# Norm statistics a stage ahead, square roots on ScalarE, weight packing beside the shared expert, a residual sum in the experts' stage, fp8 scaling on ScalarE

## The reference, cut to what matters

```python
# L0: cross-attention, 16 heads, then 8 experts with a capacity, top 2
Q = split_heads(query, 16) * dh ** (-0.5)
weights = softmax(einsum('bhqd,bhkd->bhqk', Q, Kh) + b + MASK_VALUE * (1.0 - valid))
out = einsum('bhqk,bhkd->bhqd', weights, Vh)
...
scores = softmax(xf @ router_w); expert_weights, top_experts = top_k(scores, 2)
out = out + y * expert_weights[:, k][:, None]        # y: gelu(xe @ w1) @ w2, per expert
...
# L1: rms norm, linear, "depool" add; then 8 gated experts (top 2) and one shared gated expert
sg = sigmoid(x @ shared_gate_w); so = silu(x @ sw_gate) * (x @ sw_up) @ sw_down
out = out + sg * so
# L2: cross-attention and self-attention, 4 experts of several layers; the norm ahead of them is an rms norm
# L3: projected attention, then a linear layer on fp8-rounded inputs and weights
```

## Time and profile before

| | us |
|---|---|
| device time, median of 3 runs (range) | 3182.69 (3179.83 to 3188.03) |
| the profiled execution, its own time | 3181.22 |
| its span | 3179.5 |
| PE busy in it | 2534.5 (80%) |
| DVE busy | 2180.8 (69%) |
| ACT busy | 1264.9 (40%) |
| POOL busy | 996.3 (31%) |

### The profile page before, as it was taken

One profiled execution on the slowest core, in us unless ns is written; L12 is line 12 of the kernel. 1 busy time (PEld: TensorE's weight loads), 2 busy tenths in 40 slices (PEclk: granted clock), 3 DMA queues, 4 the chain that ended last, 5 costly groups with the idle time before them and its releaser, 6 DMA issues. The chain is left out here.

```text
span 3179.5 us, 57281 instructions
## 1 busy us (share of the span) xinstructions
PE 2534.5 (80%) x21348; PEld 1651.8 (52%) x21348; DVE 2180.8 (69%) x5526; ACT 1264.9 (40%) x2260; POOL 996.3 (31%) x1420
## 2 busy tenths in 40 slices
PE   2997285999904497997989876886799999969972
PEld 1443263666603266886556543444466555656662
DVE  6897763666547764766678767997666545867758
ACT  1786353333212313111346654773322222256621
POOL 3442271110066170112656316874000000024330
PEclk9999597999956599998999987998899999989996
DMA  4331266221171026665721022100100000011001
GB/s 104 122 120 58 91 237 203 80 73 63 45 249 31 24 97 233 234 224 185 243 78 48 18 72 82 43 23 6 64 9 12 1 1 1 1 42 52 22 9 58
DMA packets 158167, 266.90 MB, mean 84 GB/s; under 512 B 22635, under 2 KB 106137, under 8 KB 151876
## 3 DMA queue, kind: packets, MB, share of 16 engines
q1 hardware_dynamic: 131204, 186.97, 17.8%
q0 software_dynamic: 17904, 76.23, 7.1%
q10 hardware_dynamic: 8784, 0.04, 0.2%
HBM read 175.25 MB, written 88.34 MB: 83 GB/s over the span
## 5 line engine op out<-in xcount | busy, mean ns | idle before, releaser
L1427 ACT ACTIVATE l2e_hf<-l2e_H 128x512 f32<-128x512 f32 x208 | 124.2, 597 | 376.1 <-PE l2e_H L1383 376.1
L1552 POOL TENSOR_TENSOR all_m_rstd<-all_m_sq,all_mhalf 128x8 f32<-128x8 f32 x18 | 29.6, 1646 | 551.0 <-DVE all_m_sq L1537 550.9
L731 DVE TENSOR_REDUCE l0a_mx<-l0a_S 128x2 f16<-128x512 f32 x256 | 168.3, 688 | 24.0 <-PE l0a_S L565 23.3
L1463 DVE CAST l2e_hh<-l2e_hf 128x512 f16<-128x512 f32 x208 | 88.8, 427 | 125.8 <-ACT l2e_hf L1427 110.7
L727 DVE CUSTOM_DVE_ANT_0 l2s_masked<-l2s_S,l2s_mq 128x128 f32<-128x128 f32 (+1 forms) x512 | 153.2, 349 | 19.9 <-PE l2s_S L565 19.5
L680 ACT ACTIVATE l0a_pf<-l0a_ST 128x512 f32<-128x512 f32 x256 | 146.7, 602 | 45.3 <-PE l0a_ST L579 45.0
L1383 PE MATMUL l2e_H<-l2o_hi,l2e_w 128*128 128x512 f16 x576 | 151.8, 382 | 14.9 <-DVE l2e_w L1439 14.9
L1427 ACT ACTIVATE l0e_hf<-l0e_H 128x512 f32<-128x512 f32 x128 | 76.4, 597 | 207.2 <-PE l0e_H L1383 207.2
L1383 PE MATMUL l2e_H<-l2e_hh,l2e_w 128*128 128x512 f16 x640 | 155.1, 379 | 0.0
L1383 PE MATMUL l1e_H<-l1b_hi,l1e_w 128*128 128x256 f16 (+1 forms) x936 | 144.7, 274 | 7.8 <-DMA l1e_w<-packed,all_second_weight_row 7.8
L1465 DVE TENSOR_TENSOR l2e_hl<-l2e_hf,l2e_hh 128x512 f16<-128x512 f32 x208 | 144.0, 693 | 7.2
(11 more groups left out here) (713 smaller groups left out, 7541.3 us busy)
## 6 DMA issues: line engine op xcount, KB each, us to landing
l0e_wf<-in_L_ffn_w SPq DMA_DIRECT2D x16, 1024.0 KB, 7.2
rows<-l0a_zeros SPq DMA_DIRECT2D x16, 640.0 KB, 5.9
l1u_rb<-rows SPq DMA_DIRECT2D x20, 512.0 KB, 5.2
results<-l1e_y SPq DMA_DIRECT2D x39, 256.0 KB, 3.8
l0a_kv<-in_ctx SPq DMA_DIRECT2D x16, 512.0 KB, 4.1
rows<-l0a_zeros SPq DMA_DIRECT2D x16, 512.0 KB, 4.9
l0d_p_cx<-in_ctx SPq DMA_DIRECT2D x16, 512.0 KB, 6.7
l0u_rb<-rows SPq DMA_DIRECT2D x16, 512.0 KB, 5.7
```

Source lines behind the costliest of these rows:

```text
L731: m = nc.vector.tensor_reduce(mx[h % 2][:, :, i], ps[:, :].rearrange("p (u k) -> p u k", u=TB), AX.X, ALU.max)
L1427: nc.scalar.activation(hf[q % 4][0:fn, :], pair_of(q, lay)[0][0:fn, :], lay.func, scale=1.0 / WS).then_inc(acted, 1)
L1463: nc.vector.tensor_copy(high, v).then_inc(hi_done, 1)
L1552: self.nc.gpsimd.tensor_tensor(out=(self.rstd, self.rstd2)[which][:, g], in0=(self.sq, self.sq2)[which][:, g], in1=self.g.mhalf[:, 0:self. ...
```

## The change

1. `load` works out the statistics of `l0n` on DVE at its end, waiting for x a quarter at a time, and three roots on POOL; SP no longer waits for x. `l0n` is built with `given=True`.
2. `l0a` is given `Moments`: in slots 2 and 3 of every second step from j = 6 DVE does BN_STATS of one tile of x and BN_AGGR of the one before, POOL three roots; `l0gn` is built with `given=True`.
3. `l1n` no longer packs weights. Its 8 roots go from POOL to ACT (`Sqrt`) with a reciprocal and one Newton step on DVE (`invert`, 5 small ops for each root).
4. `l1s` packs the weights of experts 4 to 7 instead: one of the four after each pair of down units, the high part on ACT, the low part on DVE behind the adds of the unit a = 0, loads and stores on SP, whose end waits for the last store.
5. `l2w` no longer adds `l2o_xin` to x on POOL; POOL does the 32 adds at the start of `l2e`, where DVE's first adds wait for them (`poured`).
6. `fp` multiplies by the scale on ACT instead of DVE, four times 128 x 2048, into two buffers.

```diff
+    def invert(self, dve, which, q):
+        if self.by_act:
+            nc, g = self.nc, slice(q * self.GQ, (q + 1) * self.GQ)
+            a, r, w = (self.sq, self.sq2)[which][:, g], (self.rstd, self.rstd2)[which][:, g], self.turn[:, g]
+            dve.wait_ge(self.rooted_in[which], q + 1)
+            self.then(dve, nc.vector.reciprocal(r, r))
+            self.then(dve, nc.vector.tensor_tensor(w, r, r, ALU.mult))
+            self.then(dve, nc.vector.tensor_tensor(w, w, a, ALU.mult))
+            self.then(dve, nc.vector.tensor_scalar(w, w, -0.5, 1.5, ALU.mult, ALU.add))
+            nc.vector.tensor_tensor(r, r, w, ALU.mult).then_inc(self.roots[which], 1)
...
             self.statistics(dve, q)
             if q >= 1:
+                self.invert(dve, 0, q - 1)
                 self.second(dve, q - 1)
             if q >= 2:
+                self.invert(dve, 1, q - 2)
                 self.apply(dve, q - 2)
         after(dve)
+        self.invert(dve, 0, 3)
         self.second(dve, 3)
         self.lo_parts(dve, 0)
+        self.invert(dve, 1, 2)
         self.apply(dve, 2)
         self.lo_parts(dve, 1)
+        self.invert(dve, 1, 3)
         self.apply(dve, 3)
...
+                for q in range(4):
+                    dve.wait_ge(x_in[q], 16)
+                    for t in range(8 * q, 8 * q + 8):
+                        moments.tile(dve, t)
+                moments.gather(dve, NT - 1)
...
+                if pack is not None:
+                    pack.begin_move(sp)
+                    pack.load(sp, 0)
+                    pack.load(sp, 1)
+                    for e in range(pack.experts):
+                        pack.store(sp, e)
+                        if e + 2 < pack.experts:
+                            pack.load(sp, e + 2)
+                    pack.end_move(sp)
...
+                for t in range(NT if pour is not None else 0):
+                    nc.gpsimd.tensor_tensor(out=g.x[:, t, :], in0=g.x[:, t, :], in1=pour[:, t, :], op=ALU.add
+                                            ).then_inc(poured, 1)
...
                             row = t - un.n * tiles
+                            if pour is not None and un.n == 0:
+                                dve.wait_ge(poured, row + 1)
...
+                    if pack is not None and a == 0:
+                        pack.lo_part(dve, un.i)
...
-                for t in range(NT if after is not None else 0):
-                    pool.wait_ge(posted, t + 1)
-                    after(pool, t)
...
-                    then(nc.vector.tensor_scalar(v, src, sc, None, ALU.mult))
...
+                    dve.wait_ge(scaled, q + 1)
...
+                def scale(q):
+                    if q >= 2:
+                        act.wait_ge(rounded, q - 1)
+                    nc.scalar.activation(y[q % 2][:, :, :], xn[:, q * GQ:(q + 1) * GQ, :], ACT.Copy,
+                                         scale=scl[:, 0:1]).then_inc(scaled, 1)
...
-            norm_stage(nc, "l0n", Norm(nc, g, g.x, xn, scale=0.25, live=0))
-            attention_stage(nc, g, "l0a", 16, io["ctx_2048"], xn, None, keys=0, clears=(g.rows0, g.rows1))
+            norm_stage(nc, "l0n", Norm(nc, g, g.x, xn, scale=0.25, live=0, given=True))
+            attention_stage(nc, g, "l0a", 16, io["ctx_2048"], xn, None, keys=0, clears=(g.rows0, g.rows1),
+                            moments=Moments(nc, g, g.x))
```

More of the change, by code:

```diff
@@ L122, in place @@
         self.normed = st.sem("n_normed")
+        if self.by_act:
+            self.rooted_in = [st.sem(f"n_rooted_in{i}") for i in range(2)]
+            self.turn = st.sb("n_turn", [P, NT])
         self.fetched = st.sem("n_fetched")
@@ L261, in on_pool @@
             self.root(pool, 1, 3)
+            return
+        if self.by_act:
+            for q in range(self.NQ):
+                before(pool, q)
             return
@@ L834, in _ @@
                                                bass.bass_isa.ReduceOp.max).then_inc(all_most, 1)
+                for q in range(3):
+                    moments.root(pool, q)
             @block.vector
@@ L1432, in _ @@
                                 convert(later[t])
+                        if pack is not None and un.a == 0:
+                            pack.hi_part(act, un.i)
             @block.vector
@@ L1589, in _ @@
                         moments.root(pool, t // Norm.GQ - 1)
-                for t in range(NT if after is not None else 0):
-                    pool.wait_ge(posted, t + 1)
-                    after(pool, t)
-                    if moments is not None and t % Norm.GQ == 7 and t // Norm.GQ:
-                        moments.root(pool, t // Norm.GQ - 1)
+                for q in range(Norm.NQ - 1 if moments is not None and prepare is None else 0):
+                    moments.root(pool, q)
             @block.tensor
@@ L2632, in _ @@
             def _(act):
-                for e in range(pack.experts if pack is not None else 0):
-                    pack.hi_part(act, e)
                 norm.on_scalar(act)
```

97 lines of the change are left out of this document (55 added, 42 removed).

## The result

The changed kernel takes 3169.98 us (median of 7, 3166.49 to 3172.06) where the kernel before, run beside it, takes 3179.83 (median of 7). The ratio is 0.9958, interval 0.9947 to 0.9969: 0.42% faster, over the 0.3% that can be told here, and inside the range of the prediction. Its profiled execution has a span of 3166.2 us (own time 3168.09) against 3179.5.

A forecast was written before the change was run, and what follows sets the result against it. Different engines bound different stages: DVE l0n and l0gn, POOL's gathers then a norm tail l1n, PE l1s, ACT l3g. Terms +0.4 -13.3 +0.9 +8.9 -8.5 +3.4 -2.4 +5.9 -5.2 sum to -9.9: 3172 us, range 3162 to 3184.

The forecast's parts named there:

- +9.8 with its tail: l0a: +8.9 us from statistics and small operations inside its steps, +0.9 for two tiles' statistics behind the last add.
- the rival that PE's idle time hides it: l0a: PE idles there too, so the statistics cost nothing; 3163 us, chance 0.15.
- the gap takes 0.29, 0.13 stay: l0a: a step's first tile of 0.42 us fills DVE's 0.29 wait for PE, so only 0.13 costs time.
- engines that lead in turn: l0a: PE leads up to one maximum, then DVE; two tiles cost 0.13 and 0.42, 0.55 us per even step.
- The tail: l1n behind DVE's last add: inversions on DVE and ACT's last root lengthen it by 5.5 us.
- I give 3.5 back: l1n: POOL's gathers run up to DVE's pause of about 8 us against 6 of cover, losing 3.5 us of gain.
- The 4.9: l1n: roots standing between POOL's gathers took 4.9 us together, which go when the roots leave POOL.
- Turn by turn: l2e's start: each DVE cast or operation on two SBUF operands waits 0.5 us for a POOL add; stage +5.9.
- the slack of 1.6: l2e: DVE's first add has about 1.6 us of slack before the fifth down tile, turning 5.5 into 3.9.
- The starvation rival: l2e: POOL's burst of adds starves DVE, PE starts 17.8 us later; 3184 us, chance 0.15.
- the rival that the start hides the adds: l2e: PE's lead over DVE hides POOL's adds, so they cost nothing; 3166 us, chance 0.12.
- about 8: l2e: its estimated cost in us if each DVE wait lasts a whole POOL add of 0.72, instead of 5.9.

The follow-up runs named there:

- e1: Changed kernel with one tile's statistics in slot 2 of every l0a step from j = 6, instead of two in every second; 3248.44 us, 0.9974 of before.
- e8: The changed kernel again, without edits, on one of the experiments' chips; 3253.45 us, 0.9991 of before.
- e2: Changed kernel with l0a's two tiles of statistics moved to slots 4 and 5, inside DVE's run; 3252.19 us (one run).
- e6: Changed kernel without the early statistics in load; l0n does its own again; 3246.28 us (one run).
- e5: Changed kernel with l1n's eight roots back on POOL, packing still in l1s; 3239.5 us (one run).
- e7: Changed kernel with l1s's packing behind both down units of the second and third pair, none after the last; 3249.22 us (one run).
- e3: Changed kernel with POOL's 32 adds back in l2w, none in l2e; 3253.00 us, 0.9998 of before.
- e4: Changed kernel with POOL's 32 adds in l2e each waiting for DVE's first-expert add to the same tile; 3248.18 us, 0.9979 of before.
- e9: Changed kernel with e1, e4, e6, e7 and l1n's roots split, three on ACT and five on POOL; 3228.49 us, 0.9913 of before.
- e12: As e9, but with all eight l1n roots on POOL between its gathers; 3230.08 us, 0.9912 of before.

## Why the prediction was right, by its own steps

**l0a, +9.8 with its tail, measured +9.4.** Right in kind, and nearer in sum than it deserves: DVE's delay shows in the stage, and the rival that PE's idle time hides it is refuted for the two tiles of a step (in e1, with the same work at other places, 5.1 of it are gone). A step costs 0.40 instead of 0.55. The step of the prediction that was off is "the gap takes 0.29, 0.13 stay": the room is 0.38, as e1's rows show, and nothing stays. The 0.6 for the small operation is 0.62. Twelve steps of 0.40 and two small operations make 6.0 us of the 9.4; 0.2 is the scatter of the early steps, and 3.2 lie behind the last copy of queries. Of these 1.3 are PE's 3.4 us at half clock, which e8 doesn't have, and 1.9 are the statistics' (one step, one small operation and the tail), as the prediction had them; the steps without scores cost nothing, as it said. So DVE's statistics cost 7.9 where 9.8 were put, and the clock, of which the prediction has no term, made up 1.5 by luck. Its picture of engines that lead in turn isn't complete: by it e2's pair of steps had to cost the tiles' own 0.8, and it cost 0.3.

**l0gn, -13.3, measured -12.9.** The neighbour l1gn was the right measure; 21.07 against its 20.74.

**load and l0n, +0.4, measured +1.2, shown by e6.** In the stated bounds. Its own row for l0n is 9.25 from start to start, where 8.7 was put.

**l1n, -8.5, measured -11.5.** The gathers went as said: every 1.25 us, none stretched as by a low part. From the start of the first gather to that of the last it is 80.4 where it was 97.4, 17.0 less; the prediction counted 17.4 (its chain had 64 intervals of 1.25 for 64 gathers, with the 63 there are it is 18.6). The tail was +5.5 in the prediction and is +5.8. What failed is the term "I give 3.5 back" for DVE's pause: no gather in this trace waits more than 0.78 us, the eight buffers cover it on this chip. Without that term the prediction reads -12.0. (On the chips of the experiments it is there: two waits of 5.4 and 2.4 us in e8.) And one thing it didn't separate, which e5 shows: packing out is the whole gain, roots on ACT are none. The 4.9 that it credited to the roots' leaving POOL's chain and the 5.5 that they cost behind it stood in the same sum without being set against each other.

**l1s, +3.4, measured +2.8.** The stage waits for the last store (e7 takes the wait away). The store took 4.5 from its issue, 0.1 less than the row of before, and was issued 0.02 behind the low part, where 0.4 had been put.

**l2w, -2.4, measured -3.7 with l2u; e3 says 3.8.** The 1.9 of the earlier trace rows is there. What was mis-sized is POOL's last root behind the burst, put at 0.5: it held the stage's end for 1.2 (its row stands with the result). The remaining 0.7 of e3's 3.8 lie ahead: the small operations of the first and third quarter took 0.49 and 0.46 beside the adds on the first chip (0.54 and 0.45 in e3) and take 0.17 now. On the first chip l2w itself is 4.7 shorter and l2u 1.0 longer.

**l2e, +5.9, measured +5.8; +6.5 by e3.** Turn by turn with 0.5 for each wait is what the rows show (0.49), and chunks at 2.00 instead of the 2.06 said. The split of the sum was off, and two errors cancelled: DVE's first add came 5.7 later in the stage than before, not 7.0 (1.5 + 5.5), and the slack of 1.6 that was to take part of it back isn't there, since the stage ended 5.8 later, as much as its first add within 0.2. The starvation rival is refuted in the changed kernel's own rows, and the rival that the start hides the adds by e3 and e4. The Trainium skill ("SBUF — State Buffer", section "SBUF: two separate sides") gives the whole instruction as the time that the other engine is locked out: there is blocking, as it says, but a cast beside adds of 0.72 waits 0.52 and a subtraction 0.41. By the whole 0.72 a chunk would take 1.03 + 1.44 = 2.47, an estimate, against the 2.00 measured; this trace decides for less than the whole. (Eight such chunks would add 3.3 to the prediction's 5.9, so that its "about 8" for this rule was too low by its own picture.)

**fp, -5.2, measured -4.8.** Four operations of 1.28 left DVE's chain; the chain is the bound behind them as well.

So the sum came out 3.8 us too small in gain (-9.9 against -13.7 in the stages), of which 3.0 are l1n's and 1.3 l2w's with l2u. Between the medians it is 9.9, the forecast's own number; that closeness is luck, since the stages' errors and the difference between executions are each of some 3 us. The forecast stood on the edge of what can be told; that it fell on the faster side is mainly l1n's and l2w's terms, and on the chips of the experiments, where l1n gains less, it would not have.

## What to carry to other kernels

Ask of each edit of a bundle what it brings by itself: the same removals with the work put at other places (e9, e12) gain 0.9% where the bundle gains 0.4% on one chip and nothing that can be told on another. Work moved beside another engine is free where an engine waits and has just the room: one tile ahead of each waiting maximum cost nothing, two in every second step 0.4 us, and 32 adds cost 5.8 to 6.5 us in one burst and at most 0.8 spread over the first expert. Read that room from start to start of the same instruction pair, with and without the wait between, since the idle time printed leaves out the overlap of rows (0.38 against 0.29 here).
